# The second norm's reciprocal root: GpSimd's power between its scatters, or VectorE's Newton steps between mask products

## The reference

```python
x = x + _L0_attn_ref(_layernorm(x, axis=-1), ...)   # linear attention with decay, 16 heads of 16
x = x + _L0_ffn_ref(_layernorm(x, axis=-1), ...)    # 64 experts, 8 per token, 512 rows of capacity each
x = x + _L1_attn_ref(_layernorm(x, axis=-1), ...)   # linear attention with decay, 16 heads of 128, gated
x = x + _L1_ffn_ref(_layernorm(x, axis=-1), ...)    # gated feed-forward, 1024 wide
```

## Time and profile before

| | us |
|---|---|
| median of 3 runs | 1449.16 (1448.83 to 1454.32) |
| the profiled execution, time | 1453.43 |
| the profiled execution, span | 1451.7 |
| TensorE busy | 1299.4 (90%) |
| VectorE busy | 1000.3 (69%) |
| ScalarE busy | 799.5 (55%) |
| GpSimd busy | 451.8 (31%) |

### The profile page before, as it was taken

The page is one execution under the profiler, slowest core; times in us unless marked ns, Lnnn a source line. Parts: engine busy times, 40 slices in busy tenths (PEclk is TensorE's granted clock), DMA queues, the critical chain, the costliest instruction groups (busy, mean ns, idle before and its releaser), DMA issues.

```text
span 1451.7 us, 28718 instructions
## 1 busy us (share of the span) xinstructions
PE 1299.4 (90%) x9260; PEld 1157.0 (80%) x9260; DVE 1000.3 (69%) x2071; ACT 799.5 (55%) x1543; POOL 451.8 (31%) x490
## 2 busy tenths in 40 slices
PE   4687772399999999769999999999999999999998
PEld 3465552388888888658989999899899999998997
DVE  5586776177777777666767668677677686676665
ACT  4222213166666666426666666666666666666664
POOL 1047677411111111244326226324252262251010
PEclk9998986699999999889999999999999999999999
DMA  8992223378989898740001001000010010010000
GB/s 311 423 357 90 90 88 107 128 257 291 301 297 303 294 302 294 253 136 26 20 15 52 1 23 44 13 28 25 14 43 7 14 51 0 29 36 1 8 1 9
DMA packets 58383, 173.67 MB, mean 120 GB/s; under 512 B 10064, under 2 KB 26960, under 8 KB 56144
## 3 DMA queue, kind: packets, MB, share of 16 engines
q1 hardware_dynamic: 35952, 103.61, 19.9%
q0 software_dynamic: 21504, 67.13, 14.9%
q10 hardware_dynamic: 864, 2.12, 0.4%
HBM read 86.83 MB, written 85.98 MB: 119 GB/s over the span
## 4 chain that ended last, share of the span: by engine, by line
PE 60%; DMA 15%; DVE 9%; SPq 6%; issue 5%; ACT 3%; POOL 1%; DVEq 0%; POOLq 0%; ACTq 0%
PE bank L794 17%; DMA experts<-in_moe_in 10%; PE bank L799 8%; PE bank L846 6%; PE bank L783 6%; PE bank L829 4%; PE bank L819 4%; SPq L365 4%; DMA y_rows<-D 3%; PE bank L887 3%; PE bank L830 2%; PE bank L820 2%; DVE experts L1503 1%; DVE experts L1516 1%; PE bank L713 1%
## 5 line engine op out<-in xcount | busy, mean ns | idle before, releaser
L794 PE MATMUL bank<-layer_r 128*128 128x256 f32 x2048 | 308.0, 288 | 9.4 <-issue 4.9
L1307 DVE TENSOR_TENSOR layer_r<-W,layer_r 128x1024 fp32r<-128x1024 f32 (+2 forms) x229 | 256.4, 1120 | 48.2 <-ACT layer_r L1127 48.2
L794 PEld LDWEIGHTS bank<-layer_r 128*128 128x128 f32 x2048 | 266.2, 191 | 14.1 <-issue 12.8
L1127 ACT ACTIVATE layer_r<-W 128x1024 fp32r<-128x1024 f32 (+2 forms) x226 | 221.7, 981 | 59.6 <-PE bank L846 37.2
L525 POOL TENSOR_TENSOR layer<-layer 128x256 f32<-128x256 f32 x120 | 87.5, 729 | 422.5 <-ACT layer L1202 422.0
L713 PE MATMUL bank<-experts_r 128*96 128x512 f32 x768 | 195.1, 403 | 4.6 <-DVE experts_r L1491 4.5
L495 POOL DMA_INDIRECT rows<-y_rows,sidx x128 | 170.0, 1328 | 55.2 <-issue 31.4
L799 PE MATMUL bank<-layer_r 128*128 128x256 f32 x1024 | 175.2, 283 | 0.0
L713 PEld LDWEIGHTS bank<-experts_r 128*96 128x96 f32 x768 | 121.8, 164 | 53.8 <-issue 8.5
L426 POOL DMA_INDIRECT y_rows<-W x128 | 127.8, 998 | 80.9 <-issue 57.9
L799 PEld LDWEIGHTS bank<-layer_r 128*128 128x128 f32 x1024 | 145.6, 192 | 0.0
(11 more groups left out here) (143 smaller groups left out, 2283.7 us busy)
## 6 DMA issues: line engine op xcount, KB each, us to landing
y_rows<-D SPq DMA_DIRECT2D x32, 1024.0 KB, 39.1
experts<-y_rows POOLq DMA_DIRECT2D x64, 512.0 KB, 4.7
y_rows<-experts SPq DMA_DIRECT2D x64, 512.0 KB, 4.5
W<-in_w SPq DMA_DIRECT2D x32, 416.0 KB, 5.1
experts<-in_moe_in SPq DMA_DIRECT2D x64, 192.0 KB, 4.8
experts<-in_moe_down SPq DMA_DIRECT2D x64, 96.0 KB, 4.4
y_rows<-W POOLq DMA_INDIRECT x128, 2.4
rows<-y_rows,sidx POOLq DMA_INDIRECT x128, 2.9
```

The source lines that it names most:

```text
L794: pe.matmul(out, Whi1[s][:, c * step + at:c * step + at + P], x_[:, c, :], start=(n == 0 and c == 0 and x_ is hi), stop=False, skip_group_ ...
L1127: nc.scalar.activation(Whi1[i % 2][:, 0:W.shape[1]], W, ACT.Copy).then_inc(S["d_whi"], 1)
L1307: return nc.vector.tensor_tensor(dst, src, hi.bitcast(F32), ALU.subtract)
```

## The change

The reciprocal root of the second norm leaves GpSimd. GpSimd's turn then holds only the scatters, 16 in a row for each batch. VectorE computes the root in `a_root`: a first guess from the bits of the variance (times -0.5 plus a constant, as integers), and three Newton steps y <- y * (1.5 - 0.5 * v * y * y). Each step is two instructions for the products, one for each tile because -0.5 * v is a pointer scalar, and one for the update. `a_mask(b, 1)` calls it ahead of each of its four parts: ahead of part 0 the guess, ahead of parts 1, 2 and 3 a step each. In turn 8, where there is no mask product, the four calls follow one another. The roots of the first norm and of the second layer stay on GpSimd.

```diff
-            def turn(b, back, send):
-                if send:
...
-                    a_scatter(pool, b - 2, range(5))
-                if back:
-                    rsqrt(pool, "a_var2", "a_rstd2", var2[:], rstd2[:], b)
-                if send:
-                    a_scatter(pool, b - 2, range(5, TB * TOPK))
-            for b in range(NB + 1):
-                turn(b, b > 0, b > 1)
+            def turn(b):
+                if b == 2:
+                    pool.wait_ge(S["low_rows_cleared"], 16 * (ROW_FILLS // 2))
+                if b == 3:
+                    pool.wait_ge(S["high_rows_cleared"], 16 * (ROW_FILLS // 2))
+                a_scatter(pool, b - 2)
+            for b in range(2, NB + 1):
+                turn(b)
...
-            def a_mask(b, n):
+            def a_mask(b, n, between=None):
                 for g in range(HQ):
+                    if between is not None:
+                        a_root(between, g)
                     h = 8 * (n // 2) + 2 * g
...
+            def a_root(b, k):
+                st = Steps(dve, S["a_root_steps"], ROOT_STEPS, b)
+                st.n = max(3 * k - 2, 0)
+                if k == 0:
+                    dve.wait_ge(S["a_var2"], b + 1)
+                    dve.sem_inc(S["dve_carrier"], 1)
+                    nc.vector.tensor_scalar(minus[:], var2[:], -0.5, None, ALU.mult).then_inc(S["a_minus"], 1)
+                    st.done(nc.vector.tensor_scalar(root[:].bitcast(I32), var2[:].bitcast(I32), -0.5, ROOT_SEED,
+                                                    ALU.mult, ALU.add))
+                    return
+                st.settled(S["dve_carrier"])
+                if k == 1:
+                    dve.wait_ge(S["a_minus"], b + 1)
+                for t in range(TB):
+                    st.done(nc.vector.scalar_tensor_tensor(out=square[:, t:t + 1], in0=root[:, t:t + 1],
+                                                           scalar=minus[:, t:t + 1], in1=root[:, t:t + 1],
+                                                           op0=ALU.mult, op1=ALU.mult))
+                st.settled()
+                if k < ROOT_TURNS:
+                    st.done(nc.vector.scalar_tensor_tensor(out=root[:], in0=square[:], scalar=1.5, in1=root[:],
+                                                           op0=ALU.add, op1=ALU.mult))
+                else:
+                    st.end()
+                    nc.vector.scalar_tensor_tensor(out=rstd2[:], in0=square[:], scalar=1.5, in1=root[:],
+                                                   op0=ALU.add, op1=ALU.mult).then_inc(S["a_rstd2"], 1)
...
                 if front:
-                    a_mask(b, 1)
+                    a_mask(b, 1, b - 1 if back else None)
+                elif back:
+                    for k in range(ROOT_TURNS + 1):
+                        a_root(b - 1, k)
...
+ROOT_TURNS = 3
+ROOT_STEPS = 3 * ROOT_TURNS
```

More of the change, by code:

```diff
@@ L48 @@
 DROPPED = 65536.0
+ROOT_SEED = float(0x5F3759DF)
 SENDS = 4
@@ L139, in build @@
         rstd2 = sb("rstd2", [P, TB])
+        minus = sb("minus", [P, TB])
+        root = sb("root", [P, TB])
+        square = sb("square", [P, TB])
         half = sb("half", [P, T // P])
@@ L270, in build @@
         a_xhat a_xT_ps a_xT a_q_ps a_k_ps a_v_ps a_q a_k a_v a_sc_ps a_prob a_pv_ps a_oT
-        a_out_ps a_x1 a_xh2 a_x2T_ps a_x2T a_log_ps a_logit a_ln_steps a_var a_rstd a_ln2_steps a_var2 a_rstd2
+        a_out_ps a_x1 a_xh2 a_x2T_ps a_x2T a_log_ps a_logit a_ln_steps a_var a_rstd a_ln2_steps a_var2 a_minus a_root_steps a_rstd2
         a_sel_steps a_ntop a_exp a_selb a_rank_ps a_pos_steps a_slot_steps a_scat zeros_ready low_rows_cleared high_rows_cleared
```

## The result

The changed kernel takes **1464.13 us** (median of 4 runs, 1461.39 to 1467.68); the kernel before, beside it, 1449.99 (1448.83 to 1454.32). The ratio is 1.0093 with an interval of 1.0063 to 1.0124: slower by 0.9%, 9 us over the forecast and 1 us over the end of its range. The profiled execution took 1461.39 (span 1459.7), the lowest of the four; the one of the kernel before lay above its median.

What follows compares the result with a forecast made beforehand. VectorE's turns in the first layer's attention stage were taken to bound it, with GpSimd waiting for VectorE. Root +10.4, clock +3.2, stall -6.4 and tail -1.3 gave +5.9 us: median 1455.1 us, range 1446 to 1463.

Steps and rivals of the forecast that it cites:

- (b): TensorE's longer wait ahead of the first attend drops its clock in two of turns 1 to 6: +3.2 us.
- Rival 1: TensorE's clock falls behind nearly every long wait, six falls at the attend of turns 1 to 6: 1461.5 us; chance 0.17.
- (a): Root's eleven small VectorE instructions inside the second mask product lengthen turns 1 to 7: +10.4 us by turn 7's end.
- The bound from below: Lowest cost of the root in the second mask product: eleven instructions at 0.08, opening pair hidden four times, 5.5 us.
- rival 2: Root in the second mask product nearly free, waits over when reached, no clock falls: 1447.0 us; chance 0.20.
- (c): VectorE's stall for GpSimd in turn 3 goes, making it like turn 4: -6.4 us.
- (d): After turn 7: no root among GpSimd's last scatters, shorter turn 8, batch 7's rows ready earlier: together -1.3 us.
- (e): Nothing for the rest: same scatter order and fill waits, ring of four row buffers holds, new tiles and semaphores cost nothing.

Runs made afterwards that it cites:

- the kernel with the filled wait: Changed kernel plus 11 idle identity matmuls on TensorE ahead of the first attend of turns 1 to 7; 1454.13 us, ratio 1.0016 to the kernel before.

## Why the prediction was wrong, step by step

**Where it failed: (b), the clock.** "Between none and six of turns 1 to 6 (turn 7 is slow already), I take two: +3.2 us". The mechanism, its place and its sign were right, the size was not: where 3.2 was forecast, filling the wait takes 7.0 us off turns 3 to 6. Two things were wrong in the step. It gave no reason for two falls but that the kernel before had lost the clock behind a similar wait in some turns and kept it in another; here four turns in a row, 3 to 6, lost it behind the attend, and the lengths of 27.27, 27.28 and 27.37 (and 27.20 to 27.27 with one step fewer) show one pattern that repeats. And the step left out the falls at the turns' ends: they stand in turns 2 to 5, where the kernel before has them in turns 2 and 5 and the kernel with the filled wait in turns 2 and 4.

What a fall costs can be read by setting the changed kernel beside the one with the filled wait. Turns 3 and 5 follow a turn that fell at its end in both, and differ by 1.4 and 1.3 us (27.15 and 25.78, 27.28 and 25.99): the fall behind the attend, a little less than the 1.6 of the forecast. Turns 4 and 6 differ by 2.2 and 2.1, because the fall at the end of the turn before, worth 0.8, goes too. So the price of one fall was about right, and the number of falls was not.

Rival 1, at 0.17, had the kind of loss, but not its make-up: its 9.6 are six falls at 1.6, and four came behind the attend, with two more at the turns' ends. That its 1461.5 lies 2.6 from the measured median is in part luck. The rule of the Trainium skill that stood beside that rival (page "TensorE: Matmul & The Clock Gate", section "HAM oscillation — how this bites in real kernels") agrees with the trace in kind: a wait for data in each pass, PEclk 0.87 in turns 3 to 5, and 7.0 us back when the wait is filled. It goes further than the trace where it has every pass begin slow: turns 1 and 2 waited 2.38 and 2.75 us and kept the clock.

**(a) The root, +10.4: right.** A step takes 0.45 to 0.49 (1.05 to 1.10 from part to part, less 0.60) where 0.44 was worked out, and the product 3.84 to 3.92 us where it took 2.48. With full clock on both sides the term measures 10.0 to 11.3. The bound from below (5.5), and with it rival 2, fell. The rule of the Trainium skill, page "VectorE: DVE Perf Modes", section "The DRAIN you can't avoid", by which only the count matters, falls short for these instructions: two products and an update by count alone would be 3 x 0.08 = 0.24, half of a step. No run leaves out the semaphores or the pointer operands, so it is not shown which of them makes the rest.

**(c) The stall of turn 3, -6.4: right**, shown by the kernel without steps (-6.40). That turn 3 ended at 133.33 and not near 131 is the clock again (1.4) and a stage that began 0.95 later.

**(d) The tail, -1.3: it gave 0.7.** Turn 8 came down to 18.02 (17.4 was said) and batch 7's rows wait no longer, but some scatters grew. GpSimd, columns as in the earlier trace rows:

```profile
240.56 0.97 POOL L430 DMA_INDIRECT y_rows<-W  x1 [3.34 <-DVE W L1457]
...
253.34 1.90 POOL L430 DMA_INDIRECT y_rows<-W  x1 [0.31 <-issue]
...
258.10 1.56 POOL L430 DMA_INDIRECT y_rows<-W  x1 [0.30 <-DVE W L1457]
259.97 1.97 POOL L430 DMA_INDIRECT y_rows<-W  x1 [0.30 <-issue]
...
283.01 0.97 POOL L430 DMA_INDIRECT y_rows<-W  x1 [0.30 <-issue]
```

The prediction knew one such stretch of 2 us and held it fixed; here three scatters take 1.56 to 1.97. They lie beside long instructions of VectorE, at the end of turn 8 and right behind it, but no run tells whether these are the cause.

**(e) Nothing for the rest: right for the queues.** The ring of row buffers held: no wait of VectorE's norm for the scatters shows. GpSimd only stands longer for VectorE's rows: its 16 scatters take 20.3 us and the turn 27.3.

The sum at the end of turn 7, 249.32 before and 257.59 after less turn 8 (21.73 and 18.02), is 227.59 and 239.57, +12.0. Of this the root is 10.6: the second mask products of turns 1 to 7 take 9.85 longer in sum, and the opening pair adds 0.39 in each of turns 2 and 7, where no wait hides it. The stall is -6.4; the first attend began 0.95 later for no reason in the diff (0.07 in the second trace of the changed kernel); 6.8 are left for the clock.

The expert loads start 11.25 later (274.83 to 286.08), where +5.9 was forecast. These 5.3 us are 3.6 of the clock, 0.95 of the later start, 0.6 of the tail and 0.2 of the root. The other 3.7 of the 9.0 us lie behind the stage. The stages there took 1176.9 before and 1173.6 after in these two executions, and 1173.3 to 1178.8 over all kernels, though their code is the same; what makes that difference stays open. The prediction gave them no term, yet took 4.3 us off to get from the profiled execution to the median. The difference of the medians, 14.1, has the same weakness: 1449.99 is the median of four runs, and the larger sets beside the experiments put the kernel before at 1451.91 (25 runs), 1452.73 (14) and 1452.68 (19). In the set that holds both, the changed kernel's 1463.55 lies 10.8 above 1452.73, close to the 11.25 of the expert loads.

## What to carry to other kernels

Work put between the parts of a product that another engine waits for cost its full length on the path here. Behind the last part, even without cover, it cost nothing that was measured (1445.60 against 1444.51 without the steps). When such an insertion lengthens a wait of TensorE in a loop, do not price the clock as a few falls here and there: the passes are alike, and here four in a row lost it, and two more fell at another wait. Before giving up on the change, move it one place, and fill the wait: here this turned +0.9% into -0.8%.

## What was not expected of the hardware

A wait's length alone did not decide whether the clock fell. In turns 1 to 6, waits of 1.47 to 1.86 (one step) lost it never, waits of 1.93 to 2.29 (two steps) in five of six turns, and the turn that kept it had the longest, 2.29; in the changed kernel it was kept in turn 1 through 2.38 and in turn 2 through 2.75 (2.38 and 2.83 in its second trace). TensorE's attend in turn 2:

```profile
89.59 0.64 PE L628 MATMUL bank<-layer,W 128*32 128x256 f32 x8 [2.75 <-DVE W L1328]
```

It ran in 0.64 us, at full clock. What the engine did ahead of the wait differs there (PEclk stood at 1.00 from 54 us on, while later turns came after a fall at the end of the one before). That cannot be the whole answer: with two steps the clock fell behind the attend of turn 1, at full clock since 55 us. No run was made that holds all else equal, so this stays open.
